# One kernel in which the first stage and the last attention rounds are put in another order

## Chip, cores and metric

One core of a Trainium2 chip runs the kernel. The time is the device time of the execution in microseconds (us). Engines are named as in the profile: PE (TensorE), DVE (VectorE), ACT (ScalarE), POOL (GpSimd) and SP (SyncE), which issues most of the transfers.

## What is computed

A transformer block on x (4 batches of 256 tokens, 256 channels), with float32 data:

```
decay = exp(-exp(w)) * (0.5 + 0.5 * tf)          # tf = sigmoid(sum(time_emb))
a, b  = scans over tokens, forward and backward, of a*decay + exp(k)*v and b*decay + exp(k)
h     = sigmoid(x) * (sum of both a scans + exp(u+k)*v ...) / max(sum of both b scans + ..., 1e-8) * (0.8 + 0.2*tf)
q, k, v = h @ Wq, h @ Wk, h @ Wv                 # 16 query heads, 4 key heads, 128 wide
bias  = sigmoid(q @ Wg) * (v @ Wd)               # one row per key head; only keys with bias > 0 count
x    += softmax(q k^T / sqrt(128) + bias, causal) v @ Wo
h2    = the same gated scan, with its own w and u, of x
x    += mixture of 64 experts on h2, the 8 best of each token, silu(gate) * up, down
```

k, v of the scans are the side input of a batch. The output is x, (4, 256, 256).

## The kernel before

The program is written engine by engine, each engine's list in its own order, with semaphores between them; nothing reorders it. What is read here as the order of the work is the order of the code.

**Jobs.** A gated scan of one batch is a job (c, b): c is 0 for the gated scan ahead of the attention, 1 for the one ahead of the experts, b the batch. Its parts on DVE (cond_part, from L929): part 0 makes the arguments ek and euk of the exponentials (L937, L940); ACT takes them (cond_exps, L671); part 1 makes ekv and the two forward scans of both channel halves, nf and df (L944 to L948); part 2 the backward scans (scan_back, L970) and their addition to the forward ones (join_scans, L975); POOL makes eukv (cond_products, L502) and adds euk and eukv to df and nf (cond_sums, L508); part 3 takes the reciprocal of df; part 4 makes hf, the projection's input, or for c = 1 the factor sig. The last job is (1, 3), `jobs[-1]`.

**First stage.** SP issues the loads one behind another (L385 to L400). Job (0, 0) is written out on DVE (L1107 to L1133) and gives hf of batch 0. PE then runs ten projections, `first_projs`: G (gate and delta), K, B (the bias rows turned, one small operation), Q of rounds 0 and 1, V. Each has a high part on ACT (proj_hi_part, L641) and a low part on DVE (proj_lo_part, L987), because a float32 value is kept as two fp32r numbers; they use two PSUM banks in turn, so that projection k waits for the low part of projection k - 2. The query weights are split in four groups of heads in the same way: wq_high on ACT (L742), wq_low on POOL (L550). B's rows, brow, and erow, which DVE makes of them (L1020, L1025), go through DRAM: SP stores them, loads them back to all partitions (L404 to L418), and POOL sets the part above the diagonal (masks, L515). Only then can DVE make the logits of a round (make_logits, L1027), which also wait for PE's scores.

**Rounds.** There are 16 rounds u, one for each batch and key head (NU = 16). A round takes the probabilities of its four query heads: PE turns them (turn_probs, L1490), three times four 128 x 128 pieces into the banks 5, 6 and 4; ACT copies them to pt; PE weighs the values (weigh_values); ACT copies oT; PE projects out (project_out, L1519). Around this stand the Q projection and the scores of round u + 2, whose exponentials and sums ACT takes (softmax_exp, L688), DVE's row_sums, and ACT's normalise (L680) of round u + 1. The small logits lg0 are the first 128 tokens, the large ones lg1 the other 128. Into each round two parts of the jobs from (0, 2) on are laid, an early and a late one (round_parts), and in certain rounds the routing of a batch to the experts: choice of the best eight (route_pick), the rows' places (route_key, route_slots), their weights ("hit", route_rows, L1096), ACT's copy of the rows eight times (fill_rows, L721), and POOL's indirect DMA of them to slot_rows in DRAM, eight sends for each block of 128 tokens (send_rows, L542; the last two blocks behind the rounds, L618). PE leaves project_out(14) to round 15.

**Expert stage.** SP loads 64 rows at a time from slot_rows (L432); PE turns them, multiplies by gate and up, and by down; POOL sends the results to pair_rows. The weights of the experts take the place of the query weights and of the attention's buffers as these come free: SP loads the first 22 pairs of experts, and ACT the last 10.

## Time and profile before

| | us |
|---|---|
| median of 3 runs | 524.29 |
| lowest and highest run | 521.43, 525.01 |
| the profiled execution itself | 525.55 |
| span of its trace | 523.8 |

The span is what the trace covers, from the first record to the last; times of rows are counted from its start. The granted clock of TensorE was 0.957 of 2.4 GHz in the mean. A row of a timeline gives start, duration, engine, line, operation, what it wrote and read with shapes, and in brackets how long the engine had stood idle before it, and for whom. The rows themselves are in a section below.

### The profile page before, as it was taken

Reading aid. Unit: us, or ns where it says so; the run is one execution under the profiler, and the core shown is the slowest. Engines: PE = TensorE matmul, PEld = TensorE weight load, DVE = VectorE, ACT = ScalarE, POOL = GpSimd, SP = SyncE. Lnnn points to the kernel's source line nnn. Section 1 sums busy time; section 2 is a strip of 40 time slices with the busy share of each in tenths; the row PEclk is TensorE's granted clock in tenths of the full one; section 3 lists DMA queues with packets and bytes.
Section 4 is the critical chain, followed back from the end, with each engine's and each line's share of the span. In section 5 each row is a group of like instructions: output and inputs, shape, how many; then the busy total and the mean of one; then the engine's idle time right before and its main releaser. Section 6 shows DMA issues by size and latency. Waiting matters only on the chain.

```text
span 523.8 us, 10365 instructions
## 1 busy us (share of the span) xinstructions
PE 454.5 (87%) x3069; PEld 343.3 (66%) x3069; DVE 346.8 (66%) x1206; ACT 308.9 (59%) x852; POOL 213.3 (41%) x224
## 2 busy tenths in 40 slices
PE   3487889999999889998998957869999999999474
PEld 1266677787787668786886653446777777877221
DVE  4948769559658678739859973825567777774044
ACT  4366677689586787968798670113436656665200
POOL 0323402005012265110357877403666666666700
PEclk9879899999999999999999977979999999999969
DMA  7931494100030012300029998499845555560297
GB/s 258 416 147 42 84 193 111 22 1 1 0 81 2 25 69 72 72 11 2 21 76 378 405 405 295 119 304 309 287 138 154 164 156 158 159 166 12 52 404 299
DMA packets 47318, 79.49 MB, mean 152 GB/s; under 512 B 8266, under 2 KB 31127, under 8 KB 46880
## 3 DMA queue, kind: packets, MB, share of 16 engines
q1 hardware_dynamic: 36544, 55.08, 33.7%
q0 software_dynamic: 7680, 16.93, 8.9%
q10 hardware_dynamic: 3040, 6.82, 3.9%
q8 instruction: 26, 0.43, 0.4%
q14 instruction: 28, 0.23, 0.1%
HBM read 56.54 MB, written 26.44 MB: 158 GB/s over the span
## 4 chain that ended last, share of the span: by engine, by line
PE 51%; DVE 16%; ACT 14%; DMA 8%; issue 5%; POOL 3%; SPq 2%; DVEq 0%; POOLq 0%; ACTq 0%
PE ps L1701 11%; PE ps L1403 8%; PE ps L1722 7%; PE ps L1528 6%; ACT lg L696 4%; DVE lg L1039 3%; ACT lg L639 3%; DMA pairs<-pair_rows 3%; PE ps L1451 2%; PE ps L1399 2%; PE ps L1401 2%; PE ps L1400 2%; POOL slot_rows L618 2%; DMA xrow<-slot_rows 2%; SPq L432 2%
## 5 line engine op out<-in xcount | busy, mean ns | idle before, releaser
L625 POOL DMA_INDIRECT pair_rows<-eout,dest x93 | 92.0, 989 | 61.6 <-ACT eout L639 39.7
L696 ACT ACTIVATE lg<-lg,mneg 128x128 f32<-128x128 f32 (+1 forms) x128 | 56.4, 442 | 26.1 <-DVE mneg L1039 26.0
L1701 PE MATMUL ps<-wts,xg 128*64 (+1 forms) x512 | 70.6, 341 | 1.1 <-DVE xg L1316 1.1
L546 POOL DMA_INDIRECT slot_rows<-rows,pair_slot x48 | 48.8, 1017 | 34.7 <-issue 23.6
L1701 PEld LDWEIGHTS ps<-wts,xg 128*64 128x64 f32 x512 | 52.5, 142 | 13.3 <-issue 5.5
L1528 PE MATMUL ps<-oT,wo_sb 128*128 128x256 f32 x240 | 54.4, 380 | 0.0
L1316 DVE COPY xg<-ps 128x512 f32<-128x512 f32 (+1 forms) x50 | 33.3, 666 | 29.7 <-PE ps L1403 26.1
L1528 PEld LDWEIGHTS ps<-oT,wo_sb 128*128 128x128 f32 x240 | 44.6, 190 | 6.2 <-ACT oT L639 0.7
L838 ACT ACTIVATE sact<-ps 128x192 f32<-128x192 f32 (+1 forms) x50 | 16.2, 324 | 52.0 <-PE ps L1701 50.0
L1722 PE MATMUL ps<-wts,aT 96*64 96x256 f32 (+1 forms) x256 | 46.0, 379 | 0.4 <-ACT aT L639 0.4
L639 ACT ACTIVATE lg<-lg,rinv 128x128 f32<-128x128 f32 (+1 forms) x128 | 45.9, 448 | 0.8 <-DVE rinv L1047 0.8
L1333 DVE SCALAR_TENSOR_TENSOR aact<-sact,wcol,ps 128x96 f32<-128x96 f32 x96 | 25.9, 309 | 30.4 <-issue 14.3
L1701 PE MATMUL ps<-copy_gu,xg 128*64 128x192 f32 x256 | 45.0, 329 | 0.0
L1039 DVE CUSTOM_DVE_ANT_0 lg<-ps,bm 128x128 f32<-128x128 f32 (+1 forms) x128 | 36.8, 351 | 10.0 <-PE ps L1484 9.5
L639 ACT ACTIVATE eout<-ps 128x512 f32<-128x512 f32 (+1 forms) x47 | 27.9, 594 | 23.8 <-PE ps L1722 15.9
L1399 PE MATMUL ps<-hh,wqh 128*128 128x256 f32 x128 | 38.0, 297 | 1.6 <-DVE kl L998 1.6
L506 POOL TENSOR_TENSOR eukv<-euk,vT 128x512 f32<-128x512 f32 x8 | 10.2, 1271 | 67.1 <-ACT euk L674 50.5
L1400 PE MATMUL ps<-hl,wqh 128*128 128x256 f32 x128 | 36.7, 287 | 0.0
L1401 PE MATMUL ps<-hh,wql 128*128 128x256 f32 x128 | 36.7, 287 | 0.0
L512 POOL TENSOR_TENSOR df<-df,euk 128x512 f32<-128x512 f32 x7 | 9.0, 1280 | 67.1 <-DVE df L980 67.1
L1403 PE MATMUL ps<-ident,xrow 128*128 128x128 f32 x192 | 28.0, 283 | 8.2 <-DMA xrow<-slot_rows 8.1
L1722 PEld LDWEIGHTS ps<-wts,aT 96*64 96x64 f32 x256 | 26.6, 137 | 11.7 <-ACT aT L639 0.6
(237 smaller groups left out, 1189.6 us busy)
## 6 DMA issues: line engine op xcount, KB each, us to landing
wts<-in_experts_dram SPq DMA_DIRECT2D x22, 640.0 KB, 13.9
xrow<-slot_rows SPq DMA_DIRECT2D x188, 65.0 KB
pairs<-pair_rows SPq DMA_DIRECT2D x16, 512.0 KB, 9.5
wts<-in_experts_dram ACTq DMA_DIRECT2D x10, 640.0 KB, 7.0
slot_rows<-zero SPq DMA_DIRECT2D x1, 4160.0 KB, 24.0
wT<-in_wq_t_dram SPq DMA_DIRECT2D x4, 512.0 KB, 6.9
wq_raw<-in_wq_l_dram SPq DMA_DIRECT2D x1, 2048.0 KB, 14.4
wo_sb<-in_wo_l_dram SPq DMA_DIRECT2D x1, 2048.0 KB, 20.2
```

Source lines behind the costliest of these rows:

```text
L546: nc.gpsimd.indirect_dma_start(out=slot_d, out_offset=bass.IndirectOffsetOnAxis(ap=pair_slot[:, t, k:k + 1], axis=0), in_=r[:, k, :], in_o ...
L625: nc.gpsimd.indirect_dma_start(out=pair_d, out_offset=bass.IndirectOffsetOnAxis(ap=dest[:, d:d + 1], axis=0), in_=out_rows(d), in_offset=N ...
L639: copy = lambda o_, i_, s=1.0: nc.scalar.activation(o_, i_, ACT.Copy, scale=s)
L696: ins = nc.scalar.activation(t, t, ACT.Exp, bias=mneg[:, u % 2, c:c + 1], scale=-1.0, accum_out=rsum[:, u % 2, c:c + 1])
L1039: ins = V.tensor_tensor_reduce(t, s, m, 1.0, FLT_BIG, ALU.add, ALU.min, mneg[:, u % 2, c:c + 1])
L1399: nc.tensor.matmul(o_, a[0], b_[0], start=start, stop=False)
L1400: nc.tensor.matmul(o_, a[0], b_[1], start=False, stop=False)
L1401: return nc.tensor.matmul(o_, a[1], b_[0], start=False, stop=stop)
L1403: T_ = lambda o_, i_, n=P: nc.tensor.transpose(o_, i_, ident[0:n, 0:n])
L1528: ins = nc.tensor.matmul(ps[:, 7, m * T:(m + 1) * T], wo_sb[:, n * G + h, m * P:(m + 1) * P], oT[:, h, :], start=(n == 0 and m == 0 and h ...
L1701: ins = nc.tensor.matmul(ps[h * R:(h + 1) * R, 2 + u % 2, k * I2:(k + 1) * I2], xg[u % len(xg)][:, k, cc, h * R:(h + 1) * R], moving, star ...
L1722: ins = nc.tensor.matmul(ps[h * R:(h + 1) * R, 6 + a % 2, k * C:(k + 1) * C], aT[a % 2][0:I, k, h * R:(h + 1) * R], moving, start=True, st ...
```

## The change

*First stage.* SP issues cond_b first. The sigmoid of tf is made of an exponential on ACT and of three small new DVE operations (negate and cap ahead of it, add one and reciprocal behind it; SIG_CAP is 88), and the table of the exponentials is asked for again ahead of hf, behind the sigmoids of x. The projections change places: B ahead of the second K, V's second half behind the Q's of round 1. The wql part of the first head group moves from POOL to DVE; POOL waits for the low part of the second K before its first subtraction, and makes the masks ahead of eukv. Job (0, 1)'s parts are cut up between the low parts, and its join goes behind the logits of round 1.

*Last rounds.* For job (1, 3) alone: the exponentials go ahead of the softmax of round 14; part 1 goes to the head of round 13; the backward scans behind the logits of round 15; the join behind the hits of block 4; POOL's two additions go to DVE. The normalising of round 15 is cut in two around oT, the row fill of block 5 goes into round 15, and PE's project_out(14) goes between the first and the second turn.

```diff
@@ -298,8 +298,9 @@
...
-        first_projs = [("G", 0, 0), ("K", 0, 0), ("K", 0, 1), ("B", 0, 0), ("Q", 0, 0), ("Q", 0, 1),
-                       ("V", 0, 0), ("V", 0, 1), ("Q", 1, 0), ("Q", 1, 1)]
+        first_projs = [("G", 0, 0), ("K", 0, 0), ("B", 0, 0), ("K", 0, 1), ("Q", 0, 0), ("Q", 0, 1), ("V", 0, 0),
+                       ("Q", 1, 0), ("Q", 1, 1), ("V", 0, 1)]
+        AHEAD_OF_SCORES = 7
@@ -382,9 +383,9 @@
...
+            sp.dma_start(cond_b[:], cond.rearrange("(o b) d -> o (b d)", o=1).to_broadcast([P, NB * TD])).then_inc(ld_cond, 16)
             sp.dma_start(by_batch(vT, 0), side_t[:, 0]).then_inc(ld_side[0], 16)
             sp.dma_start(wu[:], wu_t).then_inc(ld_wu, 16)
-            sp.dma_start(cond_b[:], cond.rearrange("(o b) d -> o (b d)", o=1).to_broadcast([P, NB * TD])).then_inc(ld_cond, 16)
@@ -556,11 +557,10 @@
...
-            wq_low(0)
-            pool.wait_ge(bias_ready, 1)
+            pool.wait_ge(proj_lo, order[("K", 0, 1)] + 1)
             wq_low(1)
+            masks(0)
             cond_products((0, 1))
-            masks(0)
             wq_low(2)
             cond_sums((0, 1))
             wq_low(3)
...
-                            cond_sums((c, jb))
+                            if (c, jb) != jobs[-1]:
+                                cond_sums((c, jb))
@@ -677,9 +678,9 @@
...
-            def normalise(u):
+            def normalise(u, parts=slice(0, 2)):
                 act.wait_ge(recips, u + 1)
-                for lg, c in ((lg0, 0), (lg1, G)):
+                for lg, c in ((lg0, 0), (lg1, G))[parts]:
@@ -727,12 +728,12 @@
...
-            act.wait_ge(tf_sum, 1)
-            nc.scalar.activation(tf[:], tfsum[:], ACT.Sigmoid).then_inc(tf_ready, 1)
...
+            act.wait_ge(tf_sum, 1)
+            nc.scalar.activation(tf[:], tfsum[:], ACT.Exp).then_inc(tf_ready, 1)
             cond_exps((0, 0))
@@ -749,20 +750,26 @@
...
+            act.wait_ge(dec_ready, 1)
+            nc.scalar.activation(scrap[:, 0:1], edec[:, 0, 0:1], ACT.Exp)
+            h_hi_part(0)
             wq_high(0)
-            h_hi_part(0)
-            for i, j in enumerate(first_projs[:4]):
-                proj_hi_part(j)
-                if i < 2:
-                    wq_high(i + 1)
+            proj_hi_part(("G", 0, 0))
+            wq_high(1)
+            proj_hi_part(("K", 0, 0))
+            proj_hi_part(("B", 0, 0))
+            cond_exps((0, 1))
+            proj_hi_part(("K", 0, 1))
+            proj_hi_part(("Q", 0, 0))
+            wq_high(2)
+            proj_hi_part(("Q", 0, 1))
             wq_high(3)
-            cond_exps((0, 1))
-            for j in first_projs[4:8]:
-                proj_hi_part(j)
+            proj_hi_part(("V", 0, 0))
             softmax_exp(0)
-            for j in first_projs[8:]:
-                proj_hi_part(j)
+            proj_hi_part(("Q", 1, 0))
+            proj_hi_part(("Q", 1, 1))
             normalise(0)
+            proj_hi_part(("V", 0, 1))
             act.wait_ge(wq_lo, KV - 1)
@@ -770,6 +777,8 @@
...
                     copy(pt[i][:], ps[:, turned_bank[i], :]).then_inc(pt_copied, 1)
+                    if u == NU - 1 and i == 0:
+                        fill_rows(TB * QUICK + 1)
...
                 if u == NU - 2:
-                    normalise(u + 1)
+                    normalise(u + 1, slice(0, 1))
...
                     normalise(u + 1)
-                for t in sent_in(u):
-                    if t == TB * QUICK + 1:
-                        fill_rows(t)
+                elif u == NU - 2:
+                    normalise(u + 1, slice(1, 2))
...
+                for c, jb, part in late:
+                    if part == 0 and (c, jb) == jobs[-1]:
+                        cond_exps((c, jb))
                 if u + 2 < NU:
                     softmax_exp(u + 2)
...
                 for c, jb, part in late:
-                    if part == 0:
+                    if part == 0 and (c, jb) != jobs[-1]:
                         cond_exps((c, jb))
@@ -930,7 +941,6 @@
...
-                    dve.wait_ge(cond_sum, 2 * n + 1)
+                    if (c, b) == jobs[-1]:
+                        dve.wait_ge(cond_scan, n + 1)
+                        link(V.tensor_tensor(df[:], df[:], euk[:], ALU.add))
+                    else:
+                        dve.wait_ge(cond_sum, 2 * n + 1)
...
+                    if (c, b) == jobs[-1]:
+                        dve.wait_ge(cond_uv, n + 1)
+                        link(V.tensor_tensor(nf[:], nf[:], eukv[:], ALU.add))
+                    else:
+                        dve.wait_ge(cond_sum, 2 * (n + 1))
...
+            def scan_on(c, b, cc):
+                dd = decay[:, c, cc, b:b + 1].to_broadcast([P, T])
+                V.tensor_tensor_scan(out=nf[:, cc, :], data0=dd, data1=ekv[:, cc, :], initial=0.0, op0=ALU.mult, op1=ALU.add)
+                return V.tensor_tensor_scan(out=df[:, cc, :], data0=dd, data1=ek[:, cc, :], initial=0.0, op0=ALU.mult, op1=ALU.add)
+
@@ -1107,10 +1129,13 @@
...
-            V.tensor_reduce(tfsum[:], cond_b[:].rearrange("p (b d) -> p b d", b=NB), AX.X, ALU.add).then_inc(tf_sum, 1)
+            link(V.tensor_reduce(tfsum[:], cond_b[:].rearrange("p (b d) -> p b d", b=NB), AX.X, ALU.add))
+            V.tensor_scalar(tfsum[:], tfsum[:], -1.0, SIG_CAP, ALU.mult, ALU.min).then_inc(tf_sum, 1)
...
             dve.wait_ge(tf_ready, 1)
+            link(V.tensor_scalar(tf[:], tf[:], 1.0, None, ALU.add))
+            link(V.reciprocal(tf[:], tf[:]))
@@ -1132,21 +1157,31 @@
...
-            for j in first_projs[:4]:
-                proj_lo_part(j)
+            proj_lo_part(("G", 0, 0))
+            dve.wait_ge(wq_hi, 1)
+            w = slice(0, G * HD)
+            V.tensor_tensor(wql[:, :, w], wq_raw[:, :, w], f32(wqh[:, :, w]), ALU.subtract).then_inc(wq_lo, 1)
             cond_part(0, 1, 0)
-            for j in first_projs[4:6]:
-                proj_lo_part(j)
-            cond_part(0, 1, 1)
-            for j in first_projs[6:8]:
-                proj_lo_part(j)
+            proj_lo_part(("K", 0, 0))
+            proj_lo_part(("B", 0, 0))
+            dve.wait_ge(cond_exp, 2)
+            link(V.tensor_tensor(ekv[:], ek[:], vT[:, :, T:2 * T], ALU.mult))
+            scan_on(0, 1, 0)
+            proj_lo_part(("K", 0, 1))
+            proj_lo_part(("Q", 0, 0))
+            proj_lo_part(("Q", 0, 1))
+            scan_on(0, 1, 1)
+            scan_back(0, 1, 0)
+            proj_lo_part(("V", 0, 0))
             make_logits(0)
-            scan_back(0, 1, 0)
-            for j in first_projs[8:]:
-                proj_lo_part(j)
             row_sums(0)
-            join_scans(0, 1, scan_back(0, 1, 1))
+            proj_lo_part(("Q", 1, 0))
+            proj_lo_part(("Q", 1, 1))
+            ins = scan_back(0, 1, 1)
+            link(ins)
             make_logits(1)
+            join_scans(0, 1, None)
+            proj_lo_part(("V", 0, 1))
             cond_part(0, 1, 3)
             cond_part(0, 1, 4)
@@ -1155,6 +1190,9 @@
...
+                for part in early:
+                    if part == (*jobs[-1], 1):
+                        cond_part(*part)
...
                 for part in early:
-                    cond_part(*part)
+                    if part != (*jobs[-1], 1):
+                        cond_part(*part)
...
+                if u == NU - 3:
+                    for cc in range(CC):
+                        ins = scan_back(*jobs[-1], cc)
+                    link(ins)
                 for c in routed_quick(u + 1, 2):
                     route_key(c)
                     route_slots(c)
+                if u == NU - 3:
+                    row_sums(u + 2)
+                for c in routed_quick(u + 1, 2):
                     for t in sent_in(u):
                         route_rows(t)
                 if u == NU - 3:
-                    row_sums(u + 2)
+                    join_scans(*jobs[-1], None)
                 for part in late:
-                    cond_part(*part)
+                    if part != (*jobs[-1], 2):
+                        cond_part(*part)
@@ -1487,8 +1534,8 @@
...
-            def turn_probs(u):
-                for i in range(3):
+            def turn_probs(u, parts=range(3)):
+                for i in parts:
...
             for u in range(NU):
...
-                turn_probs(u)
+                turn_probs(u, range(3) if u < NU - 1 else range(1))
...
                 if u == NU - 1:
                     project_out(u - 1)
+                    turn_probs(u, range(1, 3))
                 weigh_values(u)
```

How the lists of the engines change is shown at three places. First DVE in the first stage, behind the gate's low part, in the kernel before (kl is K's low part, ql Q's; ekv, nf, df belong to job (0, 1)):

```order
L1016 SCALAR_TENSOR_TENSOR bneg<-gb,gs 128x2x4 [waits dve_seq]
L998 TENSOR_TENSOR kl<-ps,kh 128x512 [waits proj_hi] x2
L1020 SCALAR_TENSOR_TENSOR bscan<-brow 8x128 [waits proj_hi]
L1025 TENSOR_SCALAR erow<-bscan 8x128 [waits proj_lo]
L937 TENSOR_SCALAR ek<-vT 128x512 [waits ld_side1]
L940 TENSOR_SCALAR euk<-vT,wu 128x256 x2
L994 SCALAR_TENSOR_TENSOR ql<-ps,qh 128x256 [waits proj_hi] x2
L944 TENSOR_TENSOR ekv<-ek,vT 128x512 [waits cond_exp]
L947 SCALAR_TENSOR_TENSOR nf<-decay,ekv 128x256 [waits dve_seq]
L948 SCALAR_TENSOR_TENSOR df<-decay,ek 128x256
L947 SCALAR_TENSOR_TENSOR nf<-decay,ekv 128x256
L948 SCALAR_TENSOR_TENSOR df<-decay,ek 128x256
```

And the same place in the changed kernel:

```order
L1038 SCALAR_TENSOR_TENSOR bneg<-gb,gs 128x2x4 [waits dve_seq]
L1163 TENSOR_TENSOR wql<-wq_raw,wqh 128x2x512 [waits wq_hi]
L947 TENSOR_SCALAR ek<-vT 128x512 [waits ld_side1]
L950 TENSOR_SCALAR euk<-vT,wu 128x256 x2
L1020 TENSOR_TENSOR kl<-ps,kh 128x512 [waits proj_hi]
L1042 SCALAR_TENSOR_TENSOR bscan<-brow 8x128 [waits proj_hi]
L1047 TENSOR_SCALAR erow<-bscan 8x128 [waits proj_lo]
L1168 TENSOR_TENSOR ekv<-ek,vT 128x512 [waits cond_exp]
L985 SCALAR_TENSOR_TENSOR nf<-decay,ekv 128x256 [waits dve_seq]
L986 SCALAR_TENSOR_TENSOR df<-decay,ek 128x256
L1020 TENSOR_TENSOR kl<-ps,kh 128x512 [waits proj_hi]
L1016 SCALAR_TENSOR_TENSOR ql<-ps,qh 128x256 [waits proj_hi] x2
```

The subtraction of the weights (wql) and part 0 of the job moved ahead of everything; erow went ahead of the second K; the forward scans were cut in two around the low parts.

DVE in round 13, from the weights of the routing to the first logits of round 15, before:

```order
L1080 TENSOR_TENSOR rcomb<-rrep,ri_150 128x128 [waits dve_seq]
L944 TENSOR_TENSOR ekv<-ek,vT 128x512 [waits cond_exp,dve_seq]
L947 SCALAR_TENSOR_TENSOR nf<-decay,ekv 128x256 [waits dve_seq]
L948 SCALAR_TENSOR_TENSOR df<-decay,ek 128x256
L947 SCALAR_TENSOR_TENSOR nf<-decay,ekv 128x256
L948 SCALAR_TENSOR_TENSOR df<-decay,ek 128x256
L1039 ISA lg_1_123,mneg<-ps,bm_1_103 128x128 [waits scores,bm_ready,dve_seq]
```

And in the changed kernel, where the same five rows of job (1, 3) stand behind the first two rows of the routing of that round:

```order
L1082 TENSOR_REDUCE rmx<-ps 128x2 [waits rt_logits]
L1083 TENSOR_TENSOR rl<-ps,rmx 128x128 [waits dve_seq]
L954 TENSOR_TENSOR ekv<-ek,vT 128x512 [waits cond_exp]
L985 SCALAR_TENSOR_TENSOR nf<-decay,ekv 128x256 [waits dve_seq]
L986 SCALAR_TENSOR_TENSOR df<-decay,ek 128x256
L985 SCALAR_TENSOR_TENSOR nf<-decay,ekv 128x256
L986 SCALAR_TENSOR_TENSOR df<-decay,ek 128x256
L1067 SCALAR_TENSOR_TENSOR rsum<-mneg,rsum 128x4 [waits exps,dve_seq]
L1069 RECIPROCAL rinv<-rsum 128x8 [waits dve_seq]
```

The job's part 1 left its place right ahead of the logits and stands ahead of the row sums and Q's low part.

PE in round 15, before (lg_1 are the probabilities of round 15, oT those of round 14 weighed):

```order
L1403 MATMUL ps<-ident,lg_1_123 128x128 [waits ot_copied,norms]
L1403 MATMUL ps<-ident,lg_1_123 128x128 x3
L1403 MATMUL ps<-ident,lg_1_125 128x128 [waits ot_copied,norms]
L1403 MATMUL ps<-ident,lg_1_125 128x128 x3
L1403 MATMUL ps<-ident,lg_1_125 128x128 [waits logits,norms]
L1403 MATMUL ps<-ident,lg_1_125 128x128 x3
L1528 MATMUL ps<-oT,wo_sb 128x256 [waits ot_copied]
L1528 MATMUL ps<-oT,wo_sb 128x256 x7
L1509 MATMUL ps<-pt_117,vf_107 128x512 [waits em_loaded1,pt_copied]
```

And in the changed kernel:

```order
L1450 MATMUL ps<-ident,lg_1_123 128x128 [waits ot_copied,norms]
L1450 MATMUL ps<-ident,lg_1_123 128x128 x3
L1575 MATMUL ps<-oT,wo_sb 128x256 [waits ot_copied]
L1575 MATMUL ps<-oT,wo_sb 128x256 x7
L1450 MATMUL ps<-ident,lg_1_125 128x128 [waits ot_copied,norms]
L1450 MATMUL ps<-ident,lg_1_125 128x128 x3
L1450 MATMUL ps<-ident,lg_1_125 128x128 [waits logits,norms]
L1450 MATMUL ps<-ident,lg_1_125 128x128 x3
L1556 MATMUL ps<-pt_117,vf_107 128x512 [waits em_loaded1,pt_copied]
```

The projection of round 14 moved ahead of the second and third turn. The waits are the same ones.

## Rows read from the trace of the kernel before

**Rows 1.** The page: shares of the chain that ended last
```profile
PE 51%; DVE 16%; ACT 14%; DMA 8%; issue 5%; POOL 3%; SPq 2%; DVEq 0%; POOLq 0%; ACTq 0%
```

**Rows 2.** Chain of waits, first stage and last send: start us, us, what
```profile
0.75 0.44 SPq L385
...
1.74 4.40 DMA cond_b<-in_cond_dram
...
44.68 3.62 ACT lg L696 x16
...
346.95 8.55 DMA xrow<-slot_rows
```

**Rows 3.** Timeline of DVE, first stage: start us, us, line, tile, [idle]
```profile
6.24 0.42 DVE L1110 TENSOR_REDUCE tfsum<-cond_b 128x4 f32<-128x256 f32 x1 [5.32 <-DMA cond_b<-in_cond_dram]
...
9.79 0.69 DVE L944 TENSOR_TENSOR ekv<-ek,vT 128x512 f32<-128x512 f32 x1
...
22.53 2.71 DVE L963 TENSOR_TENSOR hf<-nf,sig 128x512 f32<-128x512 f32 x1
...
30.26 0.17 DVE L1016 SCALAR_TENSOR_TENSOR bneg<-gb,gs 128x8 f32<-128x8 f32 x1
...
34.94 0.21 DVE L1025 TENSOR_SCALAR erow<-bscan 8x128 f32<-8x128 f32 x1
...
43.73 0.28 DVE L1039 CUSTOM_DVE_ANT_0 lg<-ps,bm 128x128 f32<-128x128 f32 x1
...
60.05 0.69 DVE L963 TENSOR_TENSOR hf<-nf,sig 128x512 f32<-128x512 f32 x1
```

**Rows 4.** Timeline of ACT, first stage
```profile
27.48 1.28 ACT L665 ACT_TABLE_LOAD   x1
```

**Rows 5.** Timeline of POOL, first stage and second batch
```profile
22.35 2.34 POOL L553 TENSOR_TENSOR wql<-wq_raw,wqh 128x1024 fp32r<-128x1024 f32 x1 [1.28 <-ACT wqh L639]
...
41.38 1.63 POOL L519 TENSOR_SCALAR_AFFINE_SELECT bm<-bm 128x512 f32<-128x512 f32 x2 [2.83 <-DMA bm<-bias_rows]
...
53.05 1.28 POOL L512 TENSOR_TENSOR df<-df,euk 128x512 f32<-128x512 f32 x1 [7.65 <-DVE df L980]
...
93.06 1.22 POOL L519 TENSOR_SCALAR_AFFINE_SELECT bm<-bm 128x512 f32<-128x512 f32 x2 [6.71 <-DMA bm<-bias_rows]
```

**Rows 6.** Stretches: busy time of engines, PEclk, DMA share, GB/s
```profile
30.00:31.00 1.00, 1.00 (x3) 0.80 (x3) 0.36 (x3) 0.11 (x1) 0.50 (x1) 0.50 0.04 16
...
303.00:321.00 18.00, 10.63 (x38) 7.03 (x39) 11.30 (x64) 9.24 (x12) 13.42 (x16) 0.64 1.03 406
```

**Rows 7.** Timeline of DVE, last rounds
```profile
278.12 0.69 DVE L944 TENSOR_TENSOR ekv<-ek,vT 128x512 f32<-128x512 f32 x1
...
281.32 0.29 DVE L1039 CUSTOM_DVE_ANT_0 lg<-ps,bm 128x128 f32<-128x128 f32 x1
...
284.83 0.28 DVE L1104 SCALAR_TENSOR_TENSOR hit<-key,ktop,rcomb 128x64 f32<-128x64 f32 x1
...
291.06 2.94 DVE L1104 SCALAR_TENSOR_TENSOR hit<-key,ktop,rcomb 128x64 f32<-128x64 f32 x1
```

**Rows 8.** Timelines of PE and ACT: gate projection of batch 1; last rounds
```profile
63.24 0.95 PE L1434 MATMUL ps<-wgd,hf 128*128 128x8 f32 x8
...
282.29 0.40 ACT L696 ACTIVATE lg<-lg,mneg 128x128 f32<-128x128 f32 x1 [1.76 <-DVE mneg L1039]
...
290.73 1.55 PE L1403 MATMUL ps<-ident,lg 128*128 128x128 f32 x12 [0.99 <-ACT oT L639]
```

**Rows 9.** Timeline of POOL, last rounds
```profile
288.56 1.44 POOL L546 DMA_INDIRECT slot_rows<-rows,pair_slot  x1 [0.30 <-issue]
...
291.39 1.29 POOL L512 TENSOR_TENSOR df<-df,euk 128x512 f32<-128x512 f32 x1
...
294.07 0.99 POOL L546 DMA_INDIRECT slot_rows<-rows,pair_slot  x1 [0.17 <-DVE hit L1104]
...
310.40 0.98 POOL L618 DMA_INDIRECT slot_rows<-rows,pair_slot  x1 [0.60 <-POOL rows L539]
```

13 lines of the change are left out of this document (5 added, 8 removed).

## Prediction

> **What bounds the kernel now.** I read the page's chain first: by engine it is PE 51%, DVE 16%, ACT 14%, with POOL at 3% [rows 1], so no engine holds the whole span. The expert stage after 355 us is a string of PE work which this change doesn't touch; what the change can do is to let it begin sooner. So I read the two places that are edited, and ask which wait ends last there.
>
> In the first stage the chain of waits goes from the load of cond_b (1.74 to 6.14 us) through DVE to hf, through the projections to the row of erow, and to the first softmax (3.62 us from 44.68) [rows 2, 3]. In the timeline of DVE hf takes 2.71 us, where the same shape takes 0.69 at 60.05 [rows 3]; in that of POOL a wql subtraction of 2.34 us began at 22.35, before hf was asked for at 22.53 [rows 5]. DVE was held until POOL was through. ACT loads a function table for 1.28 us at 27.48 while the gate waits [rows 4].
>
> In the last rounds DVE runs job (1,3) from ekv at 278.12 until the first logits of round 15 at 281.32, and ACT, idle for 1.76 us, begins their exponentials at 282.29 [rows 7, 8]. Later a "hit" of 0.28 us takes 2.94 at 291.06, beside POOL's df addition at 291.39 [rows 7, 9]. POOL's sends of token rows stop for that addition and its pair, and go on at 294.07; its final sends begin at 310.40 [rows 9].
>
> **First stage, step by step.** (1) cond_b is issued first, at 0.75 instead of 1.74: 1.0 us earlier, if its 4.40 us stay [rows 2]. From its landing at 6.14 to ekv at 9.79 are 3.65 us [rows 2, 3]. The sigmoid with its table leaves this stretch (1.28 us, table [rows 4]); three small DVE operations enter, some 0.2 us each as an estimate from the erow row's 0.21 [rows 3], of which one stands ahead of the exponentials and the others partly beside them. I take 0.5 us net; bounds 0 and 1.3. ekv is 1.5 us earlier.
> (2) POOL's wql for the first head group goes to DVE behind the gate, so nothing of POOL stands beside hf: 2.71 - 0.69 = 2.0 us [rows 3]. hf ends at 25.24 - 3.5 = 21.7.
> (3) In the kernel before, the gate's last operation, bneg, ends 5.2 us behind hf (30.43 against 25.24), and erow ends 4.7 us behind that, at 35.15, with waits for two K's [rows 3]. The table load goes ahead of hf, into ACT's idle time: bneg comes 5.2 - 1.3 = 3.9 us behind hf [rows 4]. Behind it DVE now has, without a wait: the wql subtraction (1024 columns; 1.3 us, at most twice the 0.69 of 512), the first part of job (0,1) (three operations over 1024 columns in all, 0.9 as an estimate from the same row), kl 0.7, bscan 0.4 and erow 0.2, in all 3.5 us in place of 4.7 [rows 3]; the second K's lo part stands behind erow now, as B's projection goes ahead of it on PE. The first K must be there for kl, 6.1 us behind hf: PE ran at 0.50, its 1.2 GHz level, at 30 us, 5 us after it had resumed [rows 6]; I leave it that slow, and it is just in time. So erow ends 7.4 us behind hf, with 0.2 for semaphores 7.6: at 29.3, 5.8 earlier. Bounds 5.0 (the subtraction at twice its price) and 6.4.
> (4) The way from erow through DRAM to the masks is 41.38 - 35.15 = 6.2 us [rows 3, 5] and stays: the masks' rows land at 35.6. DVE's own list up to V's lo part (ekv, the second K, two Q's, three pairs of scans) is 5.8 us by the prices of the 512-column rows; with some 2.1 us of waiting for the second K and the Q's, which PE can't start before the first K's lo part, it is done at 37.2, PE's scores before that. Two mask operations, 1.22 us at 93.06, took 1.63 at 41.38 beside DVE's scans [rows 5]: 0.4 more. The first logits then start at 37.6 if they don't meet, instead of 43.73 [rows 3]: 6.1 earlier.
> The Trainium skill's "SBUF — State Buffer", under "SBUF: two separate sides", says that a DVE operation with two SBUF inputs and a GpSimd one that reads SBUF exclude each other for the whole instruction. By it the four scans ahead of the logits and the two masks would take turns, and the logits start 1.1 us later than without; the hf row agrees with the rule.
> I take 0.8 us, from the 0.4 of the row and the masks' 1.22 as its two ends; the logits start 5.3 earlier.
> (5) The rest of the stage keeps its lengths but for two places. make_logits(1) goes ahead of join_scans (four operations of 256 columns, 1.6 us as an estimate from 0.69 for 512) and the second V behind the Q's of round 1. Who waits for them: job (0,1)'s join, POOL's two additions (1.28 us each [rows 5]), the reciprocal, and hf of batch 1 at 60.05 [rows 3]. That chain gains only 3 to 4 us, since the join stands behind the logits now. Before, PE began batch 1's gate projection at 63.24, 2.5 us after that hf had ended at 60.74 [rows 3, 8], since it had other work; that room is used up now, and PE gains the 5.3 all the same. I carry 5.3 to the end of round 0; bounds 3.2 (batch 1's hf decides) and 6.3 (no meeting of masks and scans). Rounds 1 to 11 are the same instructions in the same order, and engine waits alone stand in them.
>
> **Last rounds.** (6) Part 1 of job (1,3) goes ahead of the row sums into DVE's idle time of round 13: 281.32 - 278.12 = 3.2 us leave the way of the logits [rows 7]. ACT can use 1.76 of it, its idle time [rows 8]; then it is late itself. Its exponentials of round 15 start at 280.5.
> (7) In round 14 ACT normalises the small logits, copies oT, then normalises the large ones; the row fill goes behind the next pt copy. PE turned everything at 290.73 in one piece of 1.55 us, 0.99 us after it had run dry, and projected afterwards [rows 8]. Now the small turns (a third of them) and project_out(14), which needs oT alone, can stand in that gap: 0.99 us go. With step 6, PE reaches the last weighing 1.76 + 0.99 = 2.75 us earlier.
> (8) POOL loses the two additions: 291.39 to 294.07, 2.7 us [rows 9], in an unbroken row of 32 sends that starts with the first hit at 284.83 [rows 7]. That hit hardly moves (0.1): row_sums(15) goes ahead of it and waits for ACT's exponentials, which end at 280.5 + 3.6 = 284.1, and then 0.35 for itself and the slots. The send of the round before, which waited for job (1,3)'s exponentials, can begin earlier, but ends in a pause. DVE gains the 2.66 us of the held hit and pays two additions of 0.69 [rows 7]; its reciprocal has room until PE's last projection. Both ways, PE's 2.75 and POOL's 2.8, end alike. I take 2.8; bounds 1.5 (the smaller of the two falls short by the row sums' wait) and 3.6 (all of step 6).
>
> **Sum.** 5.3 + 2.8 = 8.1 us from the profiled execution's 525.55 (span 523.8 and 1.75 around it): 517.45. That execution is 1.26 above the median of the runs, 524.29; against the median I get 516.2.
>
> **Rivals.** A: batch 1's hf decides how much of the first stage is passed on (3.2 in place of 5.3): 524.29 - 3.2 - 2.8 = 518.3. For it: its chain of DVE, POOL and DVE is long and not shortened. Against: the 2.5 us of room at PE.
> B: the last rounds' gain is swallowed by the weight loads. DMA engines are full from 303 to 321 us (share 1.03, 406 GB/s) [rows 6], and these bytes get no fewer: 524.29 - 5.3 = 519.0. Against: 16 final sends from 310.40 on, at some 1.3 us each, end at 331, when the loads are through.
> C: everything goes its best way, 6.3 + 3.6: 514.4.
> D: slower. A send takes 0.99 us in POOL at 294.07, but 1.44 at 288.56, while DVE joins its scans [rows 9]. If DVE's additional SBUF work beside the sends, and a POOL that now sends without a pause, made this the rule, 32 sends would cost 0.45 each, 14.4 us: 524.29 - 8.1 + 14.4 = 530.6. It decides from 18 held sends on (8.1 / 0.45). Against: DVE's list beside the sends grows by two operations only.
> The same page, under the same heading, says that a DVE operation in a 2-port mode keeps GpSimd from writing the descriptors of its DMAs; by it a plain copy-like DVE operation beside the sends is what to look for.
> E: the change doesn't do what it says, since the row load that stands 8.55 us at 346.95 [rows 2] behind ACT's weight loads moves against them: each tenth is 0.9 us, either way. I count it in the widths.
>
> **How the numbers follow.** Forecast 0.60, A 0.16, B 0.10, C 0.09, D 0.05. A measurement of this kernel tells a change of about 1%, 5.2 us, from none: faster means below 519.05. The forecast, A and C lie below it; B lies on it. Faster: 0.60 + 0.16 + 0.09, less 0.04 for the tail of the forecast and of A, plus half of B: 0.86. Slower is D, 0.05; the rest, 0.09, is the other half of B and the tail. The range takes in C, A and B with the widths of the unknown prices: 512.5 to 520.0.
>
> **What would show it.** Right: ekv near 8.3; hf 0.7 us long, ending near 21.7; first logits near 38.4; first exponentials of round 0 some 5 us earlier; hf of batch 1 at 56 to 58; the stretch between round 1 and round 12 of unchanged length; no pause in POOL's sends from 286 on (in old time); no "hit" above 1 us in round 14; POOL's final sends beginning about 8 us earlier than 310.40. Wrong: scans or masks that take twice their time, PE at 0.50 from 50 to 60 us because it waits for batch 1's hf, sends above 1.2 us in rows, or a first row load of the expert stage that lands no earlier than before.

## The result and the profile after

The changed kernel is slower, by 0.48%: 526.96 us in the median of 19 runs, against 522.89 for the kernel before in as many runs on the same chips; the ratio is 1.0048 (95% interval 1.0025 to 1.0071), that is 2.5 us (1.3 to 3.7). I had forecast 516.2 us. Ratios leave out the runs that lie more than 1.5% above the fastest of their kernel: three of the changed kernel's here, below four of e9's twelve (526.65 to 527.66 us), and one or two elsewhere, 604.23 us in e14 among them. The profiled execution took 528.95 us (span 527.1).

The page's chain by engine has PE at 55% where it was 51%, and POOL at 0 where it was 3% [rows 1]:

```profile
PE 55%; DVE 14%; ACT 14%; DMA 9%; issue 4%; SPq 2%; ACTq 1%; DVEq 0%; POOL 0%; POOLq 0%
```

The timeline of DVE in the changed kernel answers to [rows 3]; columns are as there:

```profile
19.67 0.69 DVE L979 TENSOR_TENSOR hf<-nf,sig 128x512 f32<-128x512 f32 x1
...
28.71 0.21 DVE L1047 TENSOR_SCALAR erow<-bscan 8x128 f32<-8x128 f32 x1
...
37.03 0.99 DVE L985 TENSOR_TENSOR_SCAN nf<-decay,ekv 128x256 f32<-128x256 f32 x1
37.95 1.70 DVE L986 TENSOR_TENSOR_SCAN df<-decay,ek 128x256 f32<-128x256 f32 x1
39.58 2.81 DVE L993 TENSOR_TENSOR_SCAN nbk<-decay,ekv 128x256 f32<-128x256 f32 x1
...
43.20 0.27 DVE L1061 CUSTOM_DVE_ANT_0 lg<-ps,bm 128x128 f32<-128x128 f32 x1
...
54.48 0.29 DVE L1061 CUSTOM_DVE_ANT_0 lg<-ps,bm 128x128 f32<-128x128 f32 x1 [4.01 <-PE ps L1531]
...
65.48 0.69 DVE L979 TENSOR_TENSOR hf<-nf,sig 128x512 f32<-128x512 f32 x1
```

hf is ready at 20.36 us instead of 25.24 and erow at 28.92 instead of 35.15, both earlier than forecast. But the logits start at 43.20, only 0.53 sooner than in [rows 3]: three scans that take 0.66 us alone took 0.99, 1.70 and 2.81. Then the logits of round 1 come at 54.48, where the timeline of the kernel before has 52.89, after 4.01 us of waiting for the scores, and hf of batch 1 stands at 65.48 instead of 60.05. POOL in the same stretch [rows 5]:

```profile
33.91 2.40 POOL L554 TENSOR_TENSOR wql<-wq_raw,wqh 128x1024 fp32r<-128x1024 f32 x1 [15.68 <-DVE kl L1020]
...
37.46 1.65 POOL L507 TENSOR_TENSOR eukv<-euk,vT 128x512 f32<-128x512 f32 x1
39.06 2.77 POOL L554 TENSOR_TENSOR wql<-wq_raw,wqh 128x1024 fp32r<-128x1024 f32 x1
58.45 1.29 POOL L513 TENSOR_TENSOR df<-df,euk 128x512 f32<-128x512 f32 x1 [16.61 <-DVE df L1002]
```

The nbk scan at 39.58 ended at 42.39, 0.56 us behind POOL's wql at 39.06 + 2.77 = 41.83, close to the 0.66 that a scan takes alone: it ran when POOL was through. POOL's df addition moved from 53.05 [rows 5] to 58.45. PE in the same stretch answers to [rows 8]:

```profile
22.04 1.99 PE L1498 MATMUL ps<-hf,wk 128*128 128x256 f32 x8
...
28.42 3.78 PE L1498 MATMUL ps<-hf,wk 128*128 128x256 f32 x8 [2.23 <-DVE kl L1020]
...
48.81 3.78 PE L1491 MATMUL ps<-wv,hf 128*128 128x512 f32 x4 [3.24 <-DVE ql L1016]
52.39 1.91 PE L1531 MATMUL ps<-kf,qf 128*128 128x128 f32 x8
...
66.56 1.06 PE L1481 MATMUL ps<-wgd,hf 128*128 128x8 f32 x8 [2.81 <-DVE ql L1016]
```

The second K of batch 0 takes 3.78 us where the first, with as many matmuls, took 1.99; V's second half, at 48.81, stands ahead of the scores of round 1 at 52.39 (L1531); and the gate projection of batch 1 begins at 66.56 after 2.81 us of idle time that the kernel before did not have (the wait is put down to ql, which stands right behind hf in DVE's list).

ACT's timeline behind hf, with the table load that the change moved:

```profile
20.84 1.28 ACT L754 ACT_TABLE_LOAD   x1
22.13 0.20 ACT L754 ACTIVATE scrap<-edec 128x1 f32<-128x1 f32 x1
22.24 0.61 ACT L640 ACTIVATE hh<-hf 128x512 fp32r<-128x512 f32 x1
```

The load did not fall into ACT's idle time ahead of hf. It stands behind ACT's copy of wgd, which waits for PE, and so it began 0.48 us after hf was done; hh, the first thing made of hf, waited for it.

In the last rounds, the timeline of ACT has the exponentials of round 15 [rows 8]:

```profile
284.16 0.42 ACT L697 ACTIVATE lg<-lg,mneg 128x128 f32<-128x128 f32 x1
```

that of DVE the first hit of round 14 [rows 7]:

```profile
288.34 0.28 DVE L1126 SCALAR_TENSOR_TENSOR hit<-key,ktop,rcomb 128x64 f32<-128x64 f32 x1
```

and that of POOL the sends behind it and the first of the final ones [rows 9]:

```profile
289.44 0.98 POOL L547 DMA_INDIRECT slot_rows<-rows,pair_slot  x1 [4.96 <-DVE hit L1126]
...
311.57 0.98 POOL L619 DMA_INDIRECT slot_rows<-rows,pair_slot  x1 [0.60 <-POOL rows L540]
```

No exponential waits for DVE any more, no hit of round 14 takes more than 0.32 us, and from 289.44 on POOL sends without the two additions; ahead of it it paused for 4.96 us.

Four spans tell where most of the time goes, in every trace of this study. A is the start of the exponentials of round 0. B is from there to those of round 2. C is from the exponentials of round 12 to the final hits (the hit at 310.49 us before, 311.66 after). D is from these hits to the second of the strings of 32 gate and up matmuls that stand behind the last row load of the chain (at 362.36 before, 365.57 after). All are differences of starts in the timelines of ACT and DVE and the chain. What lies between B and C, rounds 2 to 11, is taken up in the section on why the prediction was wrong. The column on the second K is the time that PE took for it, in us.

| profile | A | B | second K | C | D | ratio of times, interval |
|---|---|---|---|---|---|---|
| before, first | 44.7 | 27.8 | one string | 75.4 | 51.9 | |
| before, again (e5) | 40.3 | 27.0 | one string | 75.5 | 51.7 | |
| last rounds only (e2) | 40.4 | 26.3 | one string | 72.8 | 55.1 | 0.9966 (0.9932 to 1.0) |
| after, first | 44.2 | 31.6 | 3.78 | 72.8 | 53.9 | 1.0048 (1.0025 to 1.0071) |
| after, again (e6) | 41.0 | 30.7 | 3.75 | 72.8 | 52.6 | |
| first stage only (e1) | 44.3 | 31.6 | 3.78 | 75.4 | 51.9 | 1.0054 (1.0025 to 1.0082) |
| after, POOL held (e3) | 38.4 | 32.5 | 1.99 | 72.8 | 52.6 | 1.0064 (1.0035 to 1.0093) |
| after, V back (e4) | 40.0 | 28.8 | 1.99 | 72.8 | 54.7 | 1.0041 (1.0015 to 1.0067) |
| after, join back (e9) | 44.2 | 28.4 | 3.78 | 72.8 | 54.3 | 0.9988 (0.9961 to 1.0015) |
| V and join back (e10) | 43.2 | 26.0 | 3.54 | 72.8 | 54.2 | 0.9948 (0.9918 to 0.9978) |
| three edits (e7) | 39.9 | 26.0 | 2.00 | 72.8 | 52.9 | 0.9939 (0.9908 to 0.9971) |
| three edits again (e14) | 42.7 | 26.0 | 3.78 | 72.8 | 53.9 | 0.9942 (0.9913 to 0.997) |
| and K's low part first (e8) | 42.1 | 26.0 | 3.37 | 72.8 | 54.1 | 0.9953 (0.9926 to 0.998) |
| three edits, old last rounds (e11) | 42.6 | 26.0 | 3.78 | 75.4 | 52.3 | 0.9972 (0.9947 to 0.9997) |
| three edits, 10 matmuls (e12) | 40.1 | 26.0 | 1.99 | 72.8 | 55.6 | 0.9987 (0.996 to 1.0014) |
| three edits, 5 matmuls (e13) | 43.0 | 26.0 | 3.78 | 72.8 | 51.4 | 0.994 (0.9913 to 0.9967) |

B is where the changed kernel loses (2.9 to 5.3 us against the three traces of the old first stage), C is where it wins (2.6), and D gives most of that back. A and B have to be read together, since what delays the exponentials of round 0 without delaying those of round 2 makes A longer and B shorter.

### The profile page after: what moved, and what is told of

The parts are those of the page before. It is cut to its first block, busy times and chain, and to the rows that moved or that the text cites. A ratio compares the mean times of both kernels' runs of the same rounds, so it can differ in the third digit from the quotient of the medians.

```text
span 527.1 us, 10367 instructions
## 1 busy us (share of the span) xinstructions
PE 460.1 (87%) x3069; PEld 346.1 (66%) x3069; DVE 349.9 (66%) x1212; ACT 307.6 (58%) x852; POOL 209.1 (40%) x221
## 4 chain that ended last, share of the span: by engine, by line
PE 55%; DVE 14%; ACT 14%; DMA 9%; issue 4%; SPq 2%; ACTq 1%; DVEq 0%; POOL 0%; POOLq 0%
PE ps L1749 12%; PE ps L1450 8%; PE ps L1770 7%; PE ps L1575 7%; ACT lg L697 4%; DMA pairs<-pair_rows 3%; ACT lg L640 3%; DMA xrow<-slot_rows 3%; DVE lg L1061 2%; PE ps L1491 2%; PE ps L1531 2%; PE ps L1446 2%; PE ps L1448 2%; PE ps L1447 2%; PE ps L1457 2%
## 5 line engine op out<-in xcount | busy, mean ns | idle before, releaser
L626 POOL DMA_INDIRECT pair_rows<-eout,dest x93 | 92.1, 990 | 61.3 <-ACT eout L640 39.8
L849 ACT ACTIVATE sact<-ps 128x192 f32<-128x192 f32 (+1 forms) x50 | 16.2, 323 | 54.0 <-PE ps L1749 52.6
L513 POOL TENSOR_TENSOR df<-df,euk 128x512 f32<-128x512 f32 x6 | 7.7, 1279 | 76.1 <-DVE df L1002 76.1
L1450 PEld LDWEIGHTS ps<-ident,xrow 128*128 128x128 f32 x192 | 21.0, 143 | 22.8 <-issue 13.0
```

Source lines behind the costliest of these rows:

```text
L626: nc.gpsimd.indirect_dma_start(out=pair_d, out_offset=bass.IndirectOffsetOnAxis(ap=dest[:, d:d + 1], axis=0), in_=out_rows(d), in_offset=N ...
L1450: T_ = lambda o_, i_, n=P: nc.tensor.transpose(o_, i_, ident[0:n, 0:n])
```

## The experiments

**The two halves by themselves.** e1 is the changed kernel with the last rounds' part of the change taken out (in the diff above, all that names `jobs[-1]`, `NU - 3`, the split of `normalise` and of `turn_probs`, and the row fill). e2 is the kernel before with that part alone.

> The changed kernel with the last rounds put back as they were; the first stage stays changed. In the trace of the changed kernel the exponentials of round 2 begin 3.3 us later than in the kernel before (75.77 against 72.49) and those of round 12 3.75 us later. Theory (the loss is all made in the first stage and round 0): 522.9 + 3.7 = 526.6 us, exponentials of round 12 near 238.9 us. Rival (the last rounds cost more than they bring, in loads that meet): 523 us or less, since that cost would be gone.

> The kernel before with the last rounds changed alone. Between the exponentials of round 12 and the final sends the changed kernel wins back 3.75 - 1.17 = 2.6 us. Theory (these 2.6 us reach the end): 520.3 us, final sends at 307.8, PE without gaps from 353. Rival (the expert weights and row loads are bound by the DMA, so that an earlier last send brings nothing): 522.9 us, with a row load before the expert string that takes 2.6 us longer.

Measured: 525.92 us (ratio 1.0054) and 521.7 (0.9966). So the whole loss is made by the first stage, and the last rounds by themselves bring 1.8 us (0 to 3.6) of the 2.6 that C shows. On top of the changed first stage they bring less, 0.3 us by the ratios (1.0054 to 1.0048); the intervals don't tell the two apart. The surprise of e2 was its first stage, which has the code of the kernel before: A 40.4 instead of 44.7. Its hf at 21.34 took 0.69 us, not the 2.71 of [rows 3].

**The same kernels again.** e5 and e6 change nothing.

> The kernel before, profiled once more. The kernel with the last rounds changed alone has the same code up to there, and yet its exponentials of round 0 begin at 40.44 and those of round 2 at 66.73, where the first profile of the kernel before has 44.68 and 72.49. Theory (the first profile was a late one: cond_b landed at 6.14, TensorE fell to 1.2 GHz from 22 to 32 us, hf stood 2.71 us beside POOL's wql): exponentials of round 0 between 40 and 42 us, of round 2 between 66.5 and 69. Rival (the first profile is the usual one): 44 to 45 and 72 to 73.

> The changed kernel, profiled once more. Its first profile and the one with the first stage alone had TensorE at 1.2 GHz while the second K of batch 0 was projected (3.78 us), two variants with the same code up to there had it at 2.4 GHz (1.99 us) after a fall that came earlier. Theory (where the fall of the clock comes is chance, and it decides): the second K takes 1.99 or 3.78; with 1.99 the second K's low part is ready near 30, POOL's eukv and wql stand elsewhere, logits of round 0 begin near 38 to 39, and the hf of batch 1 near 61; with 3.78 all stands as in the first profile (43.20, 65.48). Rival (the place of the fall is set by the code): 3.78 and 43.2 again.

They took 520.34 and 525.39 us, one execution each. The timeline of DVE in e5:

```profile
8.54 0.69 DVE L944 TENSOR_TENSOR ekv<-ek,vT 128x512 f32<-128x512 f32 x1
...
21.28 0.69 DVE L963 TENSOR_TENSOR hf<-nf,sig 128x512 f32<-128x512 f32 x1
22.86 2.42 DVE L985 TENSOR_TENSOR hl<-hf,hh 128x512 fp32r<-128x512 f32 x1 [0.89 <-ACT hh L639]
...
30.54 0.21 DVE L1025 TENSOR_SCALAR erow<-bscan 8x128 f32<-8x128 f32 x1
```

and its timeline of POOL:

```profile
22.39 2.35 POOL L553 TENSOR_TENSOR wql<-wq_raw,wqh 128x1024 fp32r<-128x1024 f32 x1 [2.56 <-ACT wqh L639]
```

The profile from which I predicted was a late one. Here cond_b's work reaches ekv at 8.54 instead of 9.79, hf is through before POOL's wql begins at 22.39, and the hold falls on the next operation, hl, with 2.42 us, of which 1.3 lie beside the table load of ACT. erow ends at 30.75, not 35.15. Against this execution the changed kernel's erow is 1.8 us earlier, not 6.2. In e6 the second K was slow again (3.75 us), but the scans met less of POOL's work, and logits began at 40.07: the same order of instructions gives 40.1 or 43.2. Across the table the second K took 1.99 to 2.00 us in four of the thirteen profiles with the changed first stage and 3.4 to 3.8 in nine. e7 and e14 below are one and the same kernel, with 2.00 in one execution and 3.78 in the other. So the rival of e6, that its place is set by the code, fails, and so does my theory there that it alone decides.

**POOL held.** e3 makes POOL wait:

```diff
             masks(0)
+            pool.wait_ge(logits, 3)
             cond_products((0, 1))
```

> The changed kernel, but POOL waits for the logits of round 0 before eukv of job (0,1) and what is behind it. In the changed kernel four scans of DVE at 37.0 to 42.4 took 0.99, 1.70, 2.81 and 0.66 us beside POOL's eukv (1.65) and wql (2.77 at 39.06); alone they take 0.66. Theory (the two engines shut each other out of SBUF): the scans take 0.66 each, logits of round 0 begin at 39.8 instead of 43.20, and the whole kernel is 3.4 us faster, 523.5. Rival 1 (the scans are slow for another reason): they stay at 1 to 2.8 us, 527.0. Rival 2 (the scans are quick but the hf of batch 1, which waits for POOL's additions, keeps its place near 65): 526 to 527.

Its timeline of DVE:

```profile
33.97 0.68 DVE L986 TENSOR_TENSOR_SCAN nf<-decay,ekv 128x256 f32<-128x256 f32 x1
...
35.15 1.10 DVE L994 TENSOR_TENSOR_SCAN nbk<-decay,ekv 128x256 f32<-128x256 f32 x1
...
37.46 0.28 DVE L1062 CUSTOM_DVE_ANT_0 lg<-ps,bm 128x128 f32<-128x128 f32 x1
```

Here the worst scan takes 1.10 us (two still meet the masks, 1.05 and 1.10, which is the meeting I had priced), and the logits begin at 37.46. Not all of that is the hold: the second K also ran in 1.99 us in this execution, and e4, without a hold but with a quick second K, has scans of 0.67 and logits at 38.18. e14 below is the better comparison, since it has the hold and a second K at the place and of the length of the changed kernel's (28.42, 3.78 us): its logits begin at 40.01 instead of 43.20, and the theory had said 39.8. The mechanism is right, yet the time of e3 is 525.51 us, ratio 1.0064: rival 2. B grew to 32.5, and what was won ahead of the logits of round 0 was lost before those of round 2.

**V and the join.** e4 puts V's second half back ahead of the Q's of round 1, e9 the join ahead of the logits of round 1, e10 both:

```diff
-                       ("Q", 1, 0), ("Q", 1, 1), ("V", 0, 1)]
+                       ("V", 0, 1), ("Q", 1, 0), ("Q", 1, 1)]
...
             proj_hi_part(("V", 0, 0))
+            proj_hi_part(("V", 0, 1))
             softmax_exp(0)
...
-            proj_hi_part(("V", 0, 1))
...
             make_logits(0)
+            proj_lo_part(("V", 0, 1))
             row_sums(0)
...
-            proj_lo_part(("V", 0, 1))
```

```diff
+            join_scans(0, 1, None)
             make_logits(1)
-            join_scans(0, 1, None)
```

> The changed kernel with V's second half projected ahead of the Q's of round 1 again, its high part on ACT ahead of the exponentials of round 0, its low part on DVE behind the logits of round 0. In the changed kernel V stands at 48.81 for 3.78 us between the low parts of Q (done at 49.3) and the scores of round 1 (52.59); the join of job (0,1), and with it hf of batch 1 (65.48), waits for these logits. Theory (V's place is what delays hf of batch 1): scores of round 1 near 49.5, hf of batch 1 near 62.2, kernel 3.3 us faster, 523.7. Rival (V's 1.9 us must be done anyway and PE is the bound): scores at 49.5 but exponentials of round 2 unchanged within 1 us, 526 to 527.

> The changed kernel with the join of job (0,1) ahead of the logits of round 1 again, nothing else. The logits of round 1 wait for scores that end near 54.3 (first profile) or 50.3 (second one), and DVE stands idle ahead of them from 50.5 or 47.4 on, so the join (1.6 us) fits in that wait. Theory (the join's place is a good part of what delays hf of batch 1): POOL's first addition 4 us earlier than in the changed kernel (17 us behind the start of the exponentials of round 0 would be 14.3 there; here 7 to 8), hf of batch 1 and the exponentials of round 2 2 to 4 us earlier against those of round 0 (30.7 and 31.6 us in the two profiles of the changed kernel), the kernel 522 to 524. Rival (V's place alone is what counts, PE having the scores of round 1 and what follows still to do): below 1 us gained, 525 to 527.

> The kernel of the three edits without the hold of POOL: V and the join are back in their old places, POOL goes on to eukv and wql as in the changed kernel. Theory (the hold is worth little by itself, since the additions of job (0,1) wait for eukv, and DVE's scans are caught in some executions only): 520.3 to 521.5, exponentials of round 2 26 us behind those of round 0, scans above 0.7 us where they stand beside POOL. Rival (DVE and POOL shutting each other out is the main loss): 523 or more.

Either edit shortens B by 2 to 3 us, both bring it to 26.0, less than in the kernel before. The two halves of B tell the edits apart. From the exponentials of round 1 to those of round 2 it takes 11.5 or 11.6 us in all eleven traces with the join in its old place, and 14.5 to 14.7 in all five with it behind the logits. From round 0 to round 1 it takes 16.2 to 18.1 us with V's second half moved, and 14.1 to 14.5 with it back, against 14.7 to 16.3 in the old first stage.

In times: V alone 1.0041, hardly a gain; the join alone 0.9988, some 3 us; both 0.9948, 5.2 us better than the changed kernel. Not all that V shortens in B is won, since ACT, which now copies V's second half ahead of the exponentials of round 0, waits for PE's V there. In the changed kernel the exponentials start 0.95 us behind the first logits, in e14 they start 2.66 us behind. Counted to the exponentials of round 2 (A + B), the traces with both edits stand at 65.9 to 69.2 us, those of the old first stage at 66.7, 67.2 and 72.5, those of the changed kernel at 71.7 and 75.8: the two edits take the loss away, but no trace shows that the first stage is then quicker than it was.

V alone disappointed because PE then waited for hf of batch 1, as its timeline shows:

```profile
45.23 1.25 PE L1531 MATMUL ps<-kf,qf 128*128 128x128 f32 x8 [2.38 <-DVE ql L1016]
...
59.63 1.73 PE L1481 MATMUL ps<-wgd,hf 128*128 128x8 f32 x8 [3.05 <-DVE ql L1016]
61.21 3.76 PE L1491 MATMUL ps<-wv,hf 128*128 128x512 f32 x4
```

and the stretches around it (busy time of PE and its load, DVE, ACT, POOL; PEclk; DMA share; GB/s):

```profile
55.00:60.00 5.00, 1.95 (x7) 0.75 (x5) 4.93 (x6) 2.74 (x13) 1.82 (x2) 0.98 0.32 68
60.00:65.00 5.00, 5.00 (x13) 2.93 (x13) 1.04 (x5) 4.20 (x11) 1.27 (x1) 0.50 0.93 192
```

PE, busy for 1.95 of the 5 us ahead of 60, ran V of batch 1 in 3.76 us at a granted clock of 0.50, its 1.2 GHz level; the same projection takes 1.96 in the kernel of both edits. A late hf costs its wait and then the clock.

**The three edits.** e7 is e10 with the hold of e3; e14 repeats it; e8 also puts K's low part and erow ahead of DVE's wql subtraction and the job's first part:

```diff
             proj_lo_part(("G", 0, 0))
+            proj_lo_part(("K", 0, 0))
+            proj_lo_part(("B", 0, 0))
             dve.wait_ge(wq_hi, 1)
...
             cond_part(0, 1, 0)
-            proj_lo_part(("K", 0, 0))
-            proj_lo_part(("B", 0, 0))
```

> The changed kernel with three edits: POOL holds eukv and wql back until the logits of round 0 are made, V's second half goes back ahead of the Q's of round 1, and the join of job (0,1) goes back ahead of the logits of round 1. With V alone put back, hf of batch 1 began at 58.55 and PE, idle ahead of it, ran the next projections at 1.2 GHz (60 to 67 us), so that the exponentials of round 2 began at 68.85. Theory (hf of batch 1 is the bound, and its delay costs twice, in the wait and in the clock): the join 3 us earlier, hf of batch 1 at 56 to 57, TensorE at 2.4 GHz from 60 us, exponentials of round 2 at 65.5 to 67, 521 us. Rival (PE's work, not hf of batch 1, is the bound there): exponentials of round 2 at 68 or later, 524 to 525.

> The kernel of the three edits, and K's first low part with erow ahead of DVE's wql subtraction and of the first part of job (0,1). In the changed kernel the second K waits for that low part (PE idle for 2.23 us ahead of 28.42). Theory (the gap ahead of the second K feeds the fall of the clock and delays erow): second K begins near 26.7, erow ends near 27.2 instead of 28.9, logits of round 0 some 1.5 us earlier than in the kernel of three edits, 520 us. Rival (the masks and the scans of DVE set the logits, so that erow's time brings nothing): no difference to the kernel of three edits beyond 0.5 us, or slower, since the exponentials of job (0,1) come 1.3 us later.

> The kernel of the three edits once more, on the same chip as the one with five unused matmuls: 519.5 to 521 beside a kernel before of 522.7 to 523.4, exponentials of round 2 at 26.0 us behind those of round 0, first long string of expert work 4.0 to 4.7 us. If the exponentials of round 0 begin near 42 instead of 39.9, the second K has run at 1.2 GHz (3.4 to 3.8 us) as in the kernel with erow moved up.

e7: 520.29 us, ratio 0.9939 (0.9908 to 0.9971), 3.2 us faster than the kernel before and some 5.7 than the changed one; e14: 520.76, ratio 0.9942. It is the version to keep. Its timeline of PE:

```profile
45.07 1.16 PE L1531 MATMUL ps<-kf,qf 128*128 128x128 f32 x8 [2.59 <-DVE ql L1017]
...
56.64 0.95 PE L1481 MATMUL ps<-wgd,hf 128*128 128x8 f32 x8
```

The gate projection of batch 1 starts at 56.64 without idle time ahead of it. The fourth edit brings nothing (0.9953), although erow ended 0.5 to 1.1 us sooner: as its rival said, erow's time is worth nothing there. What the traces show in its place is ACT's wait for V ahead of the exponentials (3.66 us of idle time ahead of its copy of V in e14). The hold by itself isn't told from nothing: 0.9939 and 0.9942 with it, 0.9948 without.

**Where the last rounds' gain goes.** e11 is e7 with the old last rounds; e12 adds to e7 ten matmuls of which nothing is used, ahead of a row turning, and e13 five, by a function that the kernel has for that purpose in the rounds before (IDLE says how many there):

```diff
                 if g < len(IDLE):
                     keep_clock(IDLE[g])
+                if g == TABLE_AT + 1:
+                    pe.wait_ge(cols_read, 2)
+                    keep_clock(5)
```

(The texts of e11 and e12 count to the start of PE's turning of rows, which stands 1.46 us ahead of D's string, so that 50.4 there is 51.9 here.)

> The kernel of the three edits with the last rounds put back as in the kernel before. Seven profiles with the changed last rounds have 72.8 us from the exponentials of round 12 to the final hits, three with the old ones 75.4; but from the final hits to the third string of expert work the first have 51.1 to 53.6 us, with the first string at 1.2 GHz, the others 50.3 to 50.4. Theory (of 2.6 us won 1.4 to 3 are lost to the clock): 75.4 and 50.3 us here, first string 2.75 us long, the kernel 520.5 to 522. Rival (all 2.6 us reach the end): 522.9.

> The kernel of the three edits, and ten matmuls on PE of which nothing is used, behind the first strings of expert work, where PE was idle for most of 340 to 347 us. They add work of 4.3 us and leave nothing out. Theory (the idle time lets the clock fall to 1.2 GHz, and the first long string pays 1.3 to 2.3 us for it): the string of 32 matmuls behind the last row load takes 2.75 us instead of 4.04, from the final hits to the third string 50 to 50.8 us instead of 51.45, the kernel 1 to 2 us faster, 518.5 to 519.5. Rival (the loads set that time, and the clock only fills it): string at 2.75 and no gain, 520.3; or later by up to 1 us, if the matmuls push the turning of rows back.

> The kernel of the three edits with five unused matmuls in the place of the ten. The ten stood 8.85 us on PE (two instructions each, 0.44 us one), not the 4.3 I had reckoned, and pushed the first long string from 347 to 351.6, while it ran in 2.82 us. Five take 4.4 us, from 341.5 to 345.9, just until the last row load lands. Theory (the clock that falls in the idle time takes 1.3 to 2.3 us of what the last rounds win): string at 2.75 to 2.82 us and the second string 51.5 us behind the final hits instead of 52.9, the kernel 1 to 1.5 us faster than the kernel of the three edits beside it. Rival (the time behind the loads is set by something else): no difference beyond 0.5 us.

e11: 522.4 us, 0.9972, 1.7 us slower than e7 by the ratios, whose intervals overlap, with C 75.4 and D 52.3. In the four traces with the old last rounds D is 51.7 to 52.3, in the ten with the new ones, without added matmuls, 52.6 to 55.1 (53.8 in the mean). Stretches of the changed kernel, columns as above:

```profile
345.00:350.00 5.00, 4.39 (x46) 3.31 (x44) 3.13 (x15) 1.32 (x4) 0.98 (x1) 1.00 0.95 302
350.00:355.00 5.00, 0.96 (x6) 0.40 (x4) 2.26 (x11) 0.00 (x0) 0.98 (x1) 0.98 1.05 349
355.00:360.00 5.00, 4.04 (x23) 2.96 (x24) 1.07 (x5) 0.76 (x2) 0.00 (x0) 0.50 1.06 341
```

and of e13:

```profile
345.00:350.00 5.00, 5.00 (x21) 2.80 (x20) 0.54 (x1) 0.00 (x0) 0.00 (x0) 1.00 1.06 343
350.00:355.00 5.00, 5.00 (x54) 3.67 (x53) 2.59 (x14) 2.16 (x6) 0.00 (x0) 1.00 1.06 325
```

The last row load and the first string behind it in the chain of the changed kernel:

```profile
348.07 7.97 DMA xrow<-slot_rows
...
357.63 4.75 PE ps L1749 x32
```

in the chain of e14:

```profile
340.93 7.96 DMA xrow<-slot_rows
...
350.48 4.85 PE ps L1749 x32
```

and in e13's timeline of PE, with the unused matmuls ahead of it:

```profile
344.43 4.56 PE L1776 MATMUL ps<-x2tm,ident 128*128 128x512 f32 x10 [1.36 <-DVE to_dump L1355]
...
350.23 2.82 PE L1749 MATMUL ps<-wts,xg 128*64 128x192 f32 x32
```

In the changed kernel PE has finished the first blocks by 350 us, is busy for 0.96 us of the next five, and the string behind the load runs at 0.50: 4.75 us instead of 2.75. The half clock is not new in this stretch, only its place is. In all four traces with the old last rounds the string of 32 ahead of the one behind the load is the slow one (4.18 to 5.39 us), and the load, which lasts 8.4 us and more there, hides it. In the kernel before:

```profile
347.53 5.17 PE L1701 MATMUL ps<-wts,xg 128*64 128x192 f32 x32
```

That load landed at 355.50, and the string behind it took 2.75 us in the chain. In the changed kernel the string ahead ran in 2.82 us, at 346.22, so that PE ran out of work earlier, and the fall came on the string that nothing hides. With five unused matmuls the clock stayed at 1.00, the string took 2.82 and D fell to 51.4, 2.5 us less than in e14 beside it. With ten (e12) the string took 2.82 too, but the matmuls stood for 8.85 us, twice what I had reckoned, and it started 4 us late; 522.58 us. In the times of whole executions e13 and e14 aren't told apart: 519.81 and 520.76 us, ratios 0.994 and 0.9942. So it is shown that the clock makes D longer, and that this can be taken away; that the 2.5 us reach the end is not shown (the two spans differ by 1.7 us, 518.4 and 520.1, with equal times up to the final hits within 0.1).

## Why the prediction was wrong

**The base.** I subtracted from one execution. It was 1.26 us above the median of three runs, but 2.7 above that of 19, and in its first stage 4.3 us behind two other executions of the same code (A 44.7 against 40.3 and 40.4). What I took for removable was partly the lateness of this one: the 2.0 us of hf in step 2 came from POOL's wql beginning 0.2 us ahead of hf, and in e2 and e5 that hold fell on hl instead, half hidden.

**Steps 1 to 3 (cond_b, hf, erow).** Steps 1 and 2 were right in mechanism and near in size: ekv at 6.93 (8.3 forecast), hf 0.69 us long ending at 20.36 (21.7). Step 3 met its number, erow ending at 28.92 (29.3), partly by luck. It had put ACT's table load into idle time ahead of hf; the load ran from 20.84 to 22.12, behind hf, and bneg ended 5.4 us behind hf instead of the 3.9 of the forecast (5.2 in the kernel before). hf had come 1.3 us sooner than forecast, and bneg to erow took 3.15 us instead of 3.7. The two other executions before have erow at 30.8 and 30.9, so that against them 1.8 to 2.0 us were won, not 5.8.

**Step 4 (the logits of round 0)** failed twice; it gave them 5.3 us, and they came 0.53 us sooner. I wrote that DVE's list would be done at 37.2 and PE's scores before that. The second K, which waits for the first one's low part behind three parts of other work on DVE, began at 28.42 at half clock and ended at 32.2; in the kernel before the two K's were one string that ended by 29 in e5. So the scores began at 37.50, against 37.39 in e5: nothing won, even without the meeting of the two engines. With a quick second K and POOL held, e3's logits began at 37.46, which is the 37.6 that step 4 had without the meeting. Then I priced the meeting of DVE and POOL at 0.8 us, with the masks alone in mind. Behind the masks came eukv and wql, and DVE's second pair of scans had been pushed beside them: 0.33 + 1.04 + 2.15 = 3.5 us, and 3.4 to 3.7 us in all in four of the five traces with a slow second K and POOL not held (0.8 in e6). The Trainium skill's "SBUF — State Buffer", under "SBUF: two separate sides", says whoever of the two starts first keeps the shared ports for its whole instruction; the trace agrees, with a scan of 2.81 us that runs in the 0.56 after POOL's 2.77.

**Step 5 (the rest of the stage keeps its lengths)** is the step that decided. It carried 5.3 us to the end of round 0; in the first profile the exponentials of round 2 start 3.3 us later than before (75.77 against 72.49). B, which was 26.3 to 27.8 us in the three traces of the old first stage, is 30.7 to 31.6. I had seen the two moves and took them for free. V's second half stands between the Q's of round 1 and their scores, and it can't start until a low part that waits behind ACT's exponentials of round 0; PE, idle for 3.24 us ahead of it, does it at a granted clock of 0.50. (In e5 PE pauses at about this place too, 2.73 us ahead of 45.48, and goes on at 0.50; but V has been done by then, in 3.70 us for both halves.) The join waits behind the logits of round 1, for 4.01 us of DVE's idle time. Both are on the way of hf of batch 1. Rival A named this place and even the sign (batch 1's hf as the bound), but let it cost only part of a gain; I said of PE that it "gains the 5.3 all the same". It had 2.5 us of room and lost it, and then the clock (3.13 us for V at 67.47 instead of 1.96). e4, e9 and e10 show it: with both undone B is 26.0, and the join's part is the 3.0 us between round 1 and round 2.

Rounds 2 to 11 did keep their length in the first profiles: exponentials of round 2 to those of round 12 162.6 us before, 163.1 after. But of the five traces with the join behind the logits this is the only one that did. The others take 164.0 (e4), 164.4 (e6) and 165.0 us (e1 and e3), each by one or two rounds that are 0.4 to 2.0 us longer, while the eleven traces with the join in its old place take 162.6 to 163.4. So the first stage's lateness may cost more than B shows; why is open.

**Steps 6 to 8 (last rounds)** were right: 2.8 us forecast, C shows 2.6 (72.8 us in all twelve traces with the new last rounds), ACT's 1.76 of idle time gone, POOL's sends unbroken. What I did not carry on is D. I had looked for the swallower in the loads (B) and the row load (E); the row load took 7.97 instead of 8.55 us, and it landed 44.4 us behind the final hits where it was 45.0 before. The loss is TensorE's clock on the string behind the row load, which was no term of mine: 4.75 us instead of 2.75.

**Rival D** (slower) was not it: sends above 1.2 us stay single ones (1.47 and 1.26 in round 14). My 5 in 100 for slower was spent on one mechanism of the last rounds, while the first stage, in which nearly every engine's list was rewritten, had none.

## What to carry to other kernels

Before pricing what a reordering removes, profile the same kernel again: a stall that depends on which of two engines comes first by 0.2 us may not be there in the next execution. When work is moved behind a wait, ask what it feeds, even if it is small: a join of 1.6 us behind logits held up the exponentials of round 2 by 3, and V of batch 1 behind PE's pauses ran partly or wholly at a granted clock of 0.50. And where a kernel fills PE's idle time on purpose, a reordering that moves that idle time must move the filling too.

## What the runs showed of the hardware

TensorE's clock fell in places where the code was the same, in some executions only. From the exponentials of round 7 to those of round 8 it took 17.9 us in both first profiles and 19.9 in e1 and e3; in e1, after PE had been idle for 1.65 us until 162.21, the granted clock was 0.50 from 164 to 167 us. The weighing of values there took 4.75 us; in the changed kernel's first profile, where PE was idle for 1.36 us at the same place and the clock stayed at 1.00, it took 3.10. The stretches of e1, columns as above:

```profile
164.00:165.00 1.00, 1.00 (x3) 0.54 (x2) 1.00 (x3) 0.00 (x0) 0.00 (x0) 0.50 0.00 0
165.00:166.00 1.00, 1.00 (x2) 0.46 (x2) 1.00 (x2) 0.54 (x1) 0.00 (x0) 0.50 0.00 0
166.00:167.00 1.00, 1.00 (x3) 0.41 (x2) 0.96 (x3) 0.06 (x1) 0.00 (x0) 0.50 0.00 0
```

The changed kernel's runs spread over 521.7 to 531.93 us, those of the kernel before beside it over 520.27 to 525.01, while those of e7 cover 517.84 to 522.26. The changed kernel's fall into two groups, seven up to 524.31 and twelve from 526.7 us on; the mean granted clock is 0.954 in the first and 0.948 in the second. That fits the clock as the cause of the spread, but only two of its executions are profiled, 528.95 and 525.39 us, and neither is of the quicker group; it stays open.
